# The first x of a cross-attention and feed-forward kernel: four transfers in place of two, and 11 filling products in place of 14

## What is computed

```python
x = x + xattn(layernorm(x), ctx, ctx, ifgate_w, ifgate_b, outnorm_w)
x = x + ffn(layernorm(x), w1, w1_s, w2, w2_s, h1, h1_s, h2, h2_s, w3, w3_s)
```

## Time and profile before

| what | value |
|---|---|
| median of 3 runs | 775.72 us (775.19 to 776.27) |
| the profiled execution, its own time | 775.79 us |
| its span in the profile | 773.9 us |
| PE busy | 764.5 us, 99% of the span |
| DVE busy | 545.8 us, 71% |
| ACT busy | 381.6 us, 49% |
| HBM read and written | 53.94 MB and 8.50 MB |

### The profile page before, as it was taken

One profiled execution on the slowest core, in us unless ns is written; L12 is line 12 of the kernel. 1 busy time (PEld: TensorE's weight loads), 2 busy tenths in 40 slices (PEclk: granted clock), 3 DMA queues, 4 the chain that ended last, 5 costly groups with the idle time before them and its releaser, 6 DMA issues.

```text
span 773.9 us, 14930 instructions
## 1 busy us (share of the span) xinstructions
PE 764.5 (99%) x6170; PEld 640.6 (83%) x6170; DVE 545.8 (71%) x1294; ACT 381.6 (49%) x570; POOL 50.9 (7%) x63
## 2 busy tenths in 40 slices
PE   8999999999999999999999999999999999999997
PEld 7878888878888888878888888888889788888886
DVE  6787867586856969578675877758695684965544
ACT  3455645464554733556445564636435562445331
POOL 3300020000200011000200002000020000000000
PEclk9999999999999999999999999999999999999999
DMA  8933010501122000320005000130102100541540
GB/s 338 368 124 115 29 30 28 191 1 35 52 100 92 28 30 27 122 71 29 30 28 189 2 30 29 69 151 9 50 29 110 54 1 3 185 142 29 162 137 29
DMA packets 14615, 63.43 MB, mean 82 GB/s; under 512 B 2016, under 2 KB 2896, under 8 KB 11728
## 3 DMA queue, kind: packets, MB, share of 16 engines
q1 hardware_dynamic: 12960, 50.12, 18.7%
q0 software_dynamic: 1296, 11.53, 3.8%
q10 hardware_dynamic: 288, 0.79, 0.3%
HBM read 53.94 MB, written 8.50 MB: 81 GB/s over the span
## 4 chain that ended last, share of the span: by engine, by line
PE 85%; DVE 11%; ACT 2%; issue 1%; POOL 0%; POOLq 0%; DVEq 0%; ACTq 0%
PE ps_f L1468 24%; PE ps_f L1469 23%; DVE decay L917 8%; PE ps_f L1434 8%; PE ps_f L1435 7%; PE ps_f L1503 4%; PE ps_f L1504 4%; PE ps_a L1356 2%; PE ps_a L1379 2%; DVE decay L933 2%; PE ps_a L1246 2%; PE ps_f L1587 1%; PE ps_a L1282 1%; PE ps_f L1302 1%; PE ps_a L1407 1%
## 5 line engine op out<-in xcount | busy, mean ns | idle before, releaser
L1468 PE MATMUL ps_f<-h_hi,wgt 128*128 128x512 f32 x1024 | 401.7, 392 | 0.0
L1469 PE MATMUL ps_f<-h_lo,wgt 128*128 128x512 f32 x1024 | 398.8, 389 | 0.0
L1468 PEld LDWEIGHTS ps_f<-h_hi,wgt 128*128 128x128 f32 x1024 | 192.2, 188 | 41.6 <-issue 0.6
L1469 PEld LDWEIGHTS ps_f<-h_lo,wgt 128*128 128x128 f32 x1024 | 192.3, 188 | 38.8
L691 ACT ACTIVATE work<-ps_f,scl 128x512 f32<-128x512 f32 x128 | 87.5, 684 | 161.2 <-PE ps_f L1469 160.6
L1076 DVE TENSOR_TENSOR h_lo<-work,h_hi 128x512 fp32r<-128x512 f32 x128 | 86.5, 689 | 98.2 <-ACT h_hi L696 97.1
L1434 PE MATMUL ps_f<-h_hi,wgt 128*128 128x512 f32 x252 | 99.8, 396 | 0.0
L1435 PE MATMUL ps_f<-h_lo,wgt 128*128 128x512 f32 x252 | 98.7, 392 | 0.0
L678 ACT ACTIVATE work<-ps_f,scl 128x512 f32<-128x512 f32 x64 | 44.1, 689 | 98.2 <-PE ps_f L1435 96.3
L696 ACT ACTIVATE h_hi<-work 128x512 fp32r<-128x512 f32 x128 | 81.0, 633 | 4.1
L1067 DVE SCALAR_TENSOR_TENSOR work<-ps_f,scl,work 128x512 f32<-128x512 f32 x64 | 48.0, 750 | 47.0 <-ACT work L678 47.0
(11 more groups left out here) (195 smaller groups left out, 701.1 us busy)
## 6 DMA issues: line engine op xcount, KB each, us to landing
decay<-m_rows SPq DMA_DIRECT2D x14, 1024.0 KB, 6.1
decay<-w_cols SPq DMA_DIRECT2D x22, 512.0 KB, 4.2
wgt<-w_cols POOLq DMA_DIRECT2D x5, 1024.0 KB, 11.8
v_aug<-ctx_tok SPq DMA_DIRECT2D x8, 528.0 KB, 4.0
wgt<-w_cols POOLq DMA_DIRECT2D x2, 2048.0 KB, 14.4
x_kept<-xs SPq DMA_DIRECT2D x8, 512.0 KB, 2.6
xs<-x SPq DMA_DIRECT2D x7, 512.0 KB, 3.6
ctxT<-ctx_t SPq DMA_DIRECT2D x7, 512.0 KB, 3.3
```

The source lines that it names most:

```text
L1468: pe.matmul(ps_f[:, bank], w, moving(h_hi[layer][:, k], as_is), start=(k == 0), stop=False)
L1469: last = pe.matmul(ps_f[:, bank], w, moving(h_lo[layer][:, k], as_is), start=False, stop=(k == KH - 1))
```

## The change

The first x comes in four transfers of one quarter (128 KB) each. Quarters 0 and 2 are issued by SP, 1 and 3 by ACT. Each has a semaphore of its own, and DVE waits for each quarter before it takes its statistics. On PE, the first run of filling products has 11 products where it had 14.

```diff
-        s_x_first = [sem(f"s_x_first{n}") for n in range(W)]
+        s_x_first = [sem(f"s_x_first{n}") for n in range(Q)]
...
-            sp.dma_start(xs[0][:, 0:TILES], x[0][:, 0:TILES]).then_inc(s_x_first[0], 16)
+            for q in range(0, Q, 2):
+                sp.dma_start(xs[0][:, q], x[0][:, q]).then_inc(s_x_first[q], 16)
...
-            act.dma_start(xs[0][:, TILES:Q], x[0][:, TILES:Q]).then_inc(s_x_first[1], 16)
+            for q in range(1, Q, 2):
+                act.dma_start(xs[0][:, q], x[0][:, q]).then_inc(s_x_first[q], 16)
...
-                        dve.wait_ge(s_x_first[q // TILES], 16)
+                        dve.wait_ge(s_x_first[q], 16)
...
-            keep_clock(14)
+            keep_clock(11)
```

## The result

| | kernel before | changed kernel |
|---|---|---|
| median | 776.19 us (20 runs, 775.19 to 776.99) | 776.75 us (20 runs, 775.94 to 780.12) |
| profiled execution | 775.79 us, span 773.9 | 776.89 us, span 775.1 |

The median of the changed kernel is 0.56 us higher. Either way the changed kernel is slower by less than 0.2%, but it is on the other side of the forecast, and outside its range. Besides the median, the long end is new: of the changed kernel's 20 runs five took 777.67 us or more, up to 780.12. None of the kernel before did.

A forecast was written before the change was run, and what follows sets the result against it. PE's path at the start, filler then gates' products, was taken as the bound, not x's. 775.79 - 0.68 (three products) - 0 (four transfers) = 775.11; from the runs' median, 775.72 - 0.68 = 775.04 us, range 774.2 to 776.2.

The forecast's parts named there:

- one term of the change's cost: Start, ACT's queue: the context's issue moves 0.40 to 0.46 us, so it lands between 6.15 and 6.61.
- the cover: Gates' products, start 6.96: context early by 0.35 us; beyond that each 0.1 us later takes 0.1 from the gain.
- this rival: Context lands late, at the gates' products: landing beyond 7.64 would lose all of the gain; chance 0.03.
- The bound for the gate weights: Start: the gate weights' issue moves by 0.42 us at most, so they are placed by 6.01, early enough.
- The three products: First filler on PE: three products removed are six records at the upper clock, worth 0.68 us.
- the rule: PE's clock at the start: its change-over varies between runs, so the removed products give 0.68, in some runs up to 1.33.
- the 0.86 us of spare time: Before ACT's copy of the turned z: x's path would allow 9.66, but ACT starts at 10.52, held by PE.
- The rival of the late rise: First filler: all six removed records run at the lower clock; gain 1.3 at most, 774.4 to 774.5 us; chance 0.16.
- The four transfers: First x in quarters: DVE's statistics end 0.4 us earlier, but this is worth 0 in the total.
- D: How much earlier DVE ends its first statistics: -0.1 to 0.5 us, taken as 0.4, worth 0.
- The low clock: Rival, around 34 us: PE's low-clock stretch comes earlier, onto the 33-column products; 776.7 us; chance 0.12.
- The covers further down: After the start: scan waits for ACT, second x lands at 8.5 before DVE's 8.95, later filler stays off the chain.

The follow-up runs named there:

- experiment 2: The changed kernel (x in quarters) with 14 filling products at the start in place of 11: 776.62 us, 0.20 above the kernel before.
- experiment 3: Kernel before with 11 filling products and only ACT's half of x split, so the context is issued at 1.74: 776.73 us, 0.31 above the kernel before.
- experiment 7: Kernel before with 11 filling products and a 16 KB transfer (the scales) issued by ACT ahead of the context: 779.88 us, 3.7 above the kernel before.
- experiment 11: x in halves, the 16 KB transfer ahead of the context, 24 filling products at the start in place of 11: 780.40 us.
- experiment 15: Experiment 11 with 13 and 19 filling products in later runs for 18 and 24, restoring PE's instruction count: 778.74 us.
- experiment 16: Experiment 1 with ACT waiting for DVE's clearing before it issues the context, no transfer more: 777.55 us, 1.4 above the kernel before.
- experiment 1: Kernel before, x still in halves, with only the first filler cut from 14 products to 11: 775.19 us, 1.23 below the kernel before.
- experiment 4: Kernel before with 11 filling products and only SP's half of x split, context issued at 1.25 as before: 775.98 us, 0.44 below the kernel before.
- experiment 6: The changed kernel with ACT's queue in the order quarter 1, context, quarter 3: 776.22 us, 0.06 above the kernel before.
- experiment 9: x in halves, 11 filling products, SP's second x issued one place earlier, at 1.73: 775.52 us, 0.82 below the kernel before.
- experiment 13: Experiment 1 with 21 filling products in the third run of filler in place of 18, restoring PE's instruction count: 775.37 us (ratio 0.9992).
- experiment 5: The changed kernel with SP holding the second x back until the first context has landed: 776.26 us, 0.10 above the kernel before.
- experiment 10: The changed kernel with SP's two small constants ahead of the second x, which goes out at 3.61: 775.98 us, 0.36 below the kernel before.
- experiment 12: Experiment 10 with the gates' context products half ahead of, half behind the turning of z, in place of two filling products: 778.06 us, 1.7 above the kernel before.
- experiment 14: Experiment 12 with 23 filling products in the third run of filler, restoring PE's instruction count: 775.84 us (ratio 0.9996).

## Why the prediction was wrong

**What failed** is one term of the change's cost: "Its issue now stands behind one more, 0.40 to 0.46 us, so it lands between 6.15 (if the DMA engines are what holds it) and 6.61". I shifted the landing by at most the shift of the issue. Seven kernels issued the context at 1.7 to 1.8 and did not hold SP's large transfers back (the changed one, profiled twice, and experiments 2, 3, 7, 11, 15 and 16): it took 4.8 to 7.9 us. Six issued it at 1.25 (before, 1, 4, 6, 9, 13): 4.6 to 5.0. An issue half a microsecond later can land 3.5 us later. With the early landing gone, the cover went as I had written: PE idled, and beyond 7.64 the gain was lost. I had named this rival, and priced its turning point correctly, but gave it 0.03, because I bounded it by its own issue. The nearest row would have warned me: in the same profile the second x, just as large as the context but issued later, took 5.9 us and not 4.9. The bound for the gate weights had the same fault: placed by 6.01, I wrote, but in the changed kernel it was 6.52 and in experiment 5 7.14, where PE waited for them.

**The three products** were right in kind and too small. Experiment 1 gives 1.23 us, where I had 0.68. The part of the PE clock in that was as the rows and the rule allowed: 22 records of filler took 4.57 us in experiment 1, 5.06 in the changed kernel and 4.22 in experiment 10, with PE starting at 2.12 each time. The rate rises at another point in each execution. The Trainium skill (TensorE: Matmul & The Clock Gate, section "What's actually happening") says so, and these runs agree. In the profile of experiment 1 the gates' products started 1.02 us sooner, more than six records at the upper level, so there the rate had risen earlier than in the kernel before. ACT's copy came 1.00 us earlier (9.52 for 10.52), and there the x path held it: that is the 0.86 us of spare time, and 0.16 by which x happened to land earlier (4.55 for 4.71). The profiled execution of the kernel before was also a lucky one, 0.40 us below the median of its 20 runs; my 0.68 was read from its clock. The rival of the late rise had put this gain at 1.3 at most, closer to the measured 1.23 than my 0.68; but the kernel before has only the one profile, with the rise at 6.3 to 6.8, so what makes up the rest of the 1.23 us is not shown.

**The four transfers** also gave more than I had bounded: D was 6.12 - 5.05 = 1.07, not at most 0.5. My bound took the last landing of x, 4.91, as fixed, and let two quarters land together there, with two statistics still to take; with quarters only one has to follow the last landing. In the changed kernel DVE could start at 3.57, when the first quarter was there, and the last was there by about 4.6. A later context alone does not do this: with x in halves the statistics began at 4.34 to 4.67 with the context late (7, 11, 15, 16) and at 4.43 to 4.71 with it early (before, 1, 9, 13). But the early quarters need it: with the context at 1.25 a quarter came at 5.45 (4) or 6.76 (6). That D is worth nothing, since PE's path is the later one, was right for the changed kernel.

**The low clock** was a rival for 776.7, the measured time almost to the digit, but that is luck: the mechanism is another. In the changed kernel's profile the low stretch still lies behind the 33-column products, as these two stretches show (columns as in the earlier trace rows):

```profile
34.90:38.40 3.50, 3.50 (x34) 1.00 1.04 431
38.60:41.90 3.30, 3.30 (x13) 0.50 0.80 318
```

What happens instead is that a further low stretch can land on the gates' products when PE has idled ahead of them (experiments 7 and 16, at a cost of about 1.6 us, but not experiment 3), and neither profile of the changed kernel has it.

**The covers further down** held where they mattered, with the scan moving as ACT's copy did (0.88 and 0.87). The second x came later than I had put it, at 9.06 and not 8.5, and DVE waited 0.70 us for it; the scan waited for ACT anyway. I did not see that removing instructions from PE moves a stall near 93 us, worth 0.3 us in the changed kernel.

**What the packets show.** A DMA transfer moves in packets; the context is 128 of them, 4 KB each, and in every profile it counts as landed 0.3 to 0.6 us after the last of them ended. The number of packets on ACT's queue in each microsecond, in the profiles of three kernels (in brackets the share that SP's queue had of the 16 engines' time; as a sum of the packets' own times it can pass 100%):

| us | before, context issued at 1.25 | changed, at 1.73 | experiment 16, at 1.78 |
|---|---|---|---|
| 5 to 6 | 44 (52%) | 62 (46%) | 65 (30%) |
| 6 to 7 | 0 (99%) | 17 (78%) | 13 (89%) |
| 7 to 8 | 0 (101%) | 6 (91%) | 3 (98%) |
| 8 to 9 | 0 (104%) | 1 (104%) | 3 (100%) |

In all three SP's large transfers get going between 5 and 6 us. Issued at 1.25, the context is then nearly done: of SP's 4 KB packets 0 to 26 ended before its last one, in all six such kernels. Issued 0.5 us later, it is not, and its last packets come a few in a microsecond while SP's queue takes nearly all of the engines' time: 87 to 243 of SP's packets ended before its last one (15 in experiment 2, where it was in time). So it is not the whole context that is late, but its tail. The context still lands ahead of the second x, in the changed kernel at 8.40 against 9.06.

**What stays open** is why so few packets go out in the tail, and what decides from run to run how long it is. Both conditions are needed: issued at 1.25, the context is in time even with the second x 0.48 us behind it (9); issued at 1.74, it is in time if SP's large transfers go out later (5, 10).

**No version beats experiment 1**, 775.19 us: halves, and the shorter filler alone. The intervals of experiments 9 and 13 overlap with its own, so the order of these three is not settled.

## What to carry to other kernels

When a transfer that someone waits for shares the engines with large ones, the moment of its issue counts for much more than the shift itself: ask what it will be mixed with, and put the issue of what the chain needs ahead of a finer split of what it doesn't need. What is put behind it comes later in turn (experiment 6). Filler ahead of a wait is worth trimming only down to the landing of what is waited for, by its worst run and not by one profile. Change one thing at a time: the shorter filler was worth 1.2 us, and the split that came with it took it all and 0.6 more, though with the longer filler the same split cost only 0.2 (experiment 2).

## What the runs showed of the hardware

- An issue 0.5 us later changed the time to landing of a 512 KB transfer from 4.6 to 5.0 us (six kernels) to 4.8 to 7.9 us (seven), with other large transfers about to start on another queue; with those held back it was 5.1 to 5.3 us (experiments 5, 10, 12 and 14). It made no difference of kind whether 128 KB, 16 KB or nothing but a wait stood in front.
- After 2.5 us without work, PE's granted clock fell to its lower level for 3.3 us, while it was already working again (experiments 7 and 16); in experiment 3 it did not fall after 2.54 us without work. The weights' loads show the lower level at the start (333 ns, then 192), where the column of the granted clock prints 1.00.
- With five filling products fewer ahead of the loop PE stood for 1.8 us amid short products 80 us later (experiment 12), and adding five in another place took this away (14). With three fewer the first pass of the loop was 0.3 us longer. The Trainium skill (Runtime: NRT & Kernel Launch, section "Instruction fetch mechanics") says that an engine's program is loaded block by block and that crossing a block's edge is mostly hidden. That such an edge causes the stall is my guess; the runs show only that it depends on the count of instructions, and that it was not hidden.
